# Dilated attention in a decoder layer: the segment scores as four wide products on TensorE in place of thirty-two 32x32 ones

## The reference

```python
x = layernorm(x + dilated_attention(x))          # 16 heads of 16, segments of 64, dilation 2
x = layernorm(x + cross_attention(x, ctx))       # 16 heads, causal, keys and values from ctx
x = layernorm(x + moe(x))                        # 32 experts, top 8, capacity, silu
```

```python
g = gather(x)                                    # [B, segment, head, 32, 16]
scores = einsum('bnhqd,bnhkd->bnhqk', g, g) * hd ** -0.5
out = einsum('bnhqk,bnhkd->bnhqd', softmax(scores), g)   # scattered back, 0 elsewhere
```

## Time and profile before

| what | value |
|---|---|
| median of 3 runs | 625.38 us (624.9 to 626.18) |
| span of the profiled execution | 719.4 us |
| PE busy, share of the span | 563.9 us, 78% |
| POOL busy | 390.5 us, 54% |
| DVE busy | 368.4 us, 51% |
| ACT busy | 330.1 us, 46% |

### The profile page before, as it was taken

The page is one execution under the profiler, slowest core; times in us unless marked ns, Lnnn a source line. Parts: engine busy times, 40 slices in busy tenths (PEclk is TensorE's granted clock), DMA queues, the critical chain, the costliest instruction groups (busy, mean ns, idle before and its releaser), DMA issues.

```text
span 719.4 us, 17476 instructions
## 1 busy us (share of the span) xinstructions
PE 563.9 (78%) x5097; PEld 414.4 (58%) x5098; DVE 368.4 (51%) x1527; ACT 330.1 (46%) x1204; POOL 390.5 (54%) x599
## 2 busy tenths in 40 slices
PE   3768787888878888888306889988998888985995
PEld 2445454544555554444105777777777776774884
DVE  1537566666677566666402444444444444443453
ACT  2445555455455455456003555555555554553012
POOL 5443445545544455545551666766666666665432
PEclk9789999999999899999556999999999999998899
DMA  9999996111111111112285554555555454554994
GB/s 206 277 275 365 342 339 231 69 59 73 68 50 64 55 73 73 65 66 74 99 308 182 155 165 150 160 156 167 152 164 159 143 157 142 164 160 148 425 418 145
DMA packets 83069, 121.31 MB, mean 169 GB/s; under 512 B 13779, under 2 KB 72669, under 8 KB 80992
## 3 DMA queue, kind: packets, MB, share of 16 engines
q1 hardware_dynamic: 64128, 78.46, 36.3%
q0 software_dynamic: 14016, 38.44, 14.7%
q10 hardware_dynamic: 4896, 4.03, 1.7%
HBM read 56.07 MB, written 69.01 MB: 174 GB/s over the span
## 4 chain that ended last, share of the span: by engine, by line
PE 54%; issue 12%; ACT 12%; DVE 9%; DMA 6%; ACTq 3%; POOL 2%; SPq 1%; another core or an unknown queue 0%; DVEq 0%; POOLq 0%
PE bank L793 14%; PE bank L809 9%; ACT pr L870 7%; PE bank L611 5%; PE bank L785 5%; PE bank L601 4%; PE bank L803 3%; PE bank L661 3%; DMA out<-fin 3%; PE bank L744 2%; DMA wall<-results 2%; DVE nmax L1024 2%; PE bank L619 2%; ACTq L296 1%; DVE tg L1218 1%
## 5 line engine op out<-in xcount | busy, mean ns | idle before, releaser
L556 POOL DMA_INDIRECT results<-ys,wcol x152 | 150.1, 988 | 25.8 <-POOL pscrap L545 22.0
L530 POOL DMA_INDIRECT queues<-x,xidx x128 | 129.1, 1009 | 36.9 <-issue 36.5
L793 PE MATMUL bank<-wall,xtT 128*128 x616 | 127.1, 330 | 0.7 <-issue 0.7
L870 ACT ACTIVATE pr<-bank,nmax 128x128 f32<-128x128 f32 x256 | 90.9, 370 | 29.1 <-DVE nmax L1024 29.1
L1218 DVE SCALAR_TENSOR_TENSOR tg<-th,bank 128x96 f32<-128x96 f32 x154 | 39.1, 254 | 125.3 <-ACT th L957 96.9
L793 PEld LDWEIGHTS bank<-wall,xtT 128*128 128x128 f32 x616 | 98.4, 194 | 1.4 <-issue 1.3
L963 ACT ACTIVATE ys<-bank,wcol 128x256 f32<-128x256 f32 x152 | 71.9, 473 | 54.6 <-PE bank L809 36.6
L809 PE MATMUL bank<-wall,hT 96*128 x304 | 94.5, 392 | 0.0
L785 PE MATMUL bank<-ident,xt 128*128 128x128 f32 x310 | 63.3, 286 | 35.4 <-DMA xt<-queues 24.1
L785 PEld LDWEIGHTS bank<-ident,xt 128*128 128x128 f32 x310 | 59.0, 197 | 49.9 <-DMA xt<-queues 25.1
L876 ACT COPY prT<-bank 128x512 f32<-128x512 f32 x64 | 38.5, 601 | 88.9 <-PE bank L611 86.2
(11 more groups left out here) (178 smaller groups left out, 947.2 us busy)
## 6 DMA issues: line engine op xcount, KB each, us to landing
xt<-queues SPq DMA_DIRECT2D x162, 160.0 KB
results<-zeros SPq DMA_DIRECT2D x16, 1024.0 KB
wall<-results SPq DMA_DIRECT2D x16, 1024.0 KB, 12.7
queues<-zeros SPq DMA_DIRECT2D x32, 160.0 KB, 4.9
wall<-in_L_ffn_w_gate SPq DMA_DIRECT2D x4, 768.0 KB
wall<-in_L_ffn_w_up SPq DMA_DIRECT2D x4, 768.0 KB
wall<-in_L_ffn_w_down SPq DMA_DIRECT2D x4, 768.0 KB
results<-ys,wcol POOLq DMA_INDIRECT x152
```

The source lines that it names most:

```text
L530: pool.indirect_dma_start(xg, bass.IndirectOffsetOnAxis(ap=xidx[:, par, k:k + 1], axis=0), x2[:, par, :], None, bounds_check=last_row, oob ...
L556: pool.indirect_dma_start(yr, bass.IndirectOffsetOnAxis(ap=wcol[:, u, 1:2], axis=0), ys[:, u, :], None, bounds_check=last_y, oob_is_err=Fa ...
L793: ins = pe.matmul(bank[2 + u % 2][:, 0:2 * INTER].rearrange("p (g i) -> p g i", g=2), xtT[:, u % 2, kk, :], wall[:, bass.ds(e, GU)].rearrange(
L870: ins = act.activation(pr[:, g % 2, q, :], pS[g % 2][:, q * P:(q + 1) * P], ACT.Exp, bias=nmax[:, 4 * g + q:4 * g + q + 1], accum_out=den[ ...
```

## The change

The scores of A are built from a folded and transposed `gm`. For each half `h` of the features (128 columns), PE multiplies `gm[:, half]` as weights with `fold`, a constant of 128x64 that adds the even and the odd token rows of a segment. Because each column of `gm` is zero in one of the two, the result `[128 features, 64]` holds every feature with its own tokens. ACT copies it from PSUM to `gF`. DVE then writes `gK` in one product: the same rows spread over four blocks, each feature only in the block of its own pair (`quarter` is that 0/1 mask). ACT writes the query rows `gQ` with two scaled copies, one for even and one for odd heads (`qmask` also carries the factor of 1/4, which leaves the exponentials' `scale`). The scores are then 4 products: weights of 128 rows and 64 columns, 128 moving columns. PE folds for tile `a+1` after the logits and before keys and values of tile `a`, and waits for the copy `gF` (`fold_out`, which ACT makes between the copies of T2 and of `x1`) before the transposes of `x1`. ACT makes the query rows (`query_rows`) after `vX` and before the copy of T3. DVE's product (`spread_x`) stands in the place of `turn_x`, which goes. The constants that this needs come before the first tile; their order on POOL changes, and the four pairs of masks of `qmask` move ahead of the first `mask_x`. The products of the probabilities with `gm` (L661) stay as they are.

```diff
-FIRST_CONST = 4
-B_CONST = FIRST_CONST + 23
-N_CONST = 49
+FIRST_CONST = 4 + 15
+B_CONST = FIRST_CONST + 14
+N_CONST = 55
...
+            put(pool.tensor_tensor, fold[:, :].rearrange("p (s i) -> p s i", s=2),
+                halves[:, :, 0, :], halves[:, :, 1, :], ALU.add)
+            put(pool.memset, qmask[:, :], float(HD) ** -0.5)
+            put(pool.memset, quarter[:, :], 0.0)
+            for g in range(NG):
+                rows = slice(GR * g, GR * (g + 1))
...
+                put(pool.memset, quarter[rows, g:g + 1], 1.0)
...
+            def folded(a, par):
+                pe.wait_ge(poolA.sem, poolA.at(a, "gm"))
+                for h in range(2):
+                    ins = pe.matmul(pX[:, D + SEG * h:D + SEG * (h + 1)], gm[:, par, h * P:(h + 1) * P], fold[:, :],
+                                    start=True, stop=True)
+                ins.then_inc(peG, 1)
...
-                for j in range(PAIRS):
-                    for g in range(NG):
-                        blk32 = gT[GR * g:GR * (g + 1), j * 32:(j + 1) * 32]
-                        ins = pe.matmul(pA[GR * g:GR * (g + 1), D + j * 32:D + (j + 1) * 32], blk32, blk32,
-                                        start=True, stop=True, tile_position=(GR * g, GR * g))
+                pe.wait_ge(actG.sem, actG.at(a, "query"))
+                for h in range(2):
+                    for k in range(2):
+                        ins = pe.matmul(pA[SEG * k:SEG * (k + 1), D + h * P:D + (h + 1) * P],
+                                        gQ[:, h, k, :, :].rearrange("p k i -> p (k i)"),
+                                        gK[:, 2 * h + k, :, :].rearrange("p j i -> p (j i)"),
+                                        start=True, stop=True, tile_position=(0, SEG * k))
...
+                if a is not None and not (isinstance(a, int) and a == NB - 1):
+                    folded(a + 1, 1 - par)
...
+                        pe.wait_ge(actG.sem, actG.at(a + 1, "fold"))
...
+            def fold_out(a):
+                act.wait_ge(peG, a + 1)
+                act.copy(gF[:, :, :].rearrange("p w i -> p (w i)"), pX[:, D:D + 2 * SEG]).then_inc(actG.sem, 1)
+            def query_rows(a):
+                act.wait_ge(actG.sem, actG.at(a, "fold"))
+                for k in range(DIL):
+                    ins = act.activation(gQ[:, :, :, k, :].rearrange("p h s i -> p (h s) i"), gF[:, :, :], ACT.Copy,
+                                         scale=qmask[:, k:k + 1])
...
-            def turn_x(a, par):
-                dve.wait_ge(poolA.sem, poolA.at(a, "gm"))
-                dve.transpose(gT[:, :], gm[:, par, :]).then_inc(dveA.sem, 1)
+            def spread_x(a):
+                dve.wait_ge(actG.sem, actG.at(a, "fold"))
+                dve.tensor_tensor(gK[:, :, :, :],
+                                  gF[:, :, :].unsqueeze(2)
+                                  .to_broadcast([P, 4, 4, GR]),
+                                  quarter[:, :].unsqueeze(1).unsqueeze(3).to_broadcast([P, 4, 4, GR]),
+                                  ALU.mult).then_inc(dveA.sem, 1)
```

More of the change, by code:

```diff
@@ L218, in build @@
         actX = Steps(sem("actX"), "r a")
-        dveA = Steps(sem("dveA"), "gT max sub sum inv turn scale add stats aggr")
+        dveA = Steps(sem("dveA"), "gK max sub sum inv turn scale add stats aggr")
+        peG = sem("peG")
+        actG = Steps(sem("actG"), "fold query")
         poolA = Steps(sem("poolA"), "gm ct")
@@ L424, in _ @@
             put(pool.memset, power[:, :], -0.5)
-            assert n == FIRST_CONST
+            halves = ident[:, :].rearrange("p (s k i) -> p s k i", s=2, k=DIL)
+            put(pool.tensor_tensor, fold[:, :].rearrange("p (s i) -> p s i", s=2),
[4 more added lines that the diff above has]
+                rows = slice(GR * g, GR * (g + 1))
+                for k, most in ((0, HD - 1), (1, -HD)):
+                    put(pool.affine_select, out=qmask[rows, k:k + 1], in_=qmask[rows, k:k + 1],
+                        compare_op=ALU.is_ge, fill=0.0, base=most, pattern=[[0, 1]],
+                        channel_multiplier=-1 if k == 0 else 1)
+                put(pool.memset, quarter[rows, g:g + 1], 1.0)
+            assert n == FIRST_CONST, n
             put(pool.memset, own[:, :], 0.0)
@@ L437, in _ @@
             put(pool.memset, causal[:, :], 0.0)
-            put(pool.memset, qmask[:, :], float(HD) ** -0.5)
             put(pool.tensor_copy, identb[:, :], ident[:, :])
@@ L441, in _ @@
                 rows = slice(GR * g, GR * (g + 1))
-                for k, most in ((0, HD - 1), (1, -HD)):
-                    put(pool.affine_select, out=qmask[rows, k:k + 1], in_=qmask[rows, k:k + 1],
-                        compare_op=ALU.is_ge, fill=0.0, base=most, pattern=[[0, 1]],
-                        channel_multiplier=-1 if k == 0 else 1)
                 put(pool.affine_select, out=causal[rows, :], in_=causal[rows, :], compare_op=ALU.is_ge,
@@ L695, in step @@
                 if a is not None:
+                    if not (isinstance(a, int) and a == NB - 1):
+                        pe.wait_ge(actG.sem, actG.at(a + 1, "fold"))
                     pe.wait_ge(dveN.sem, dveN.at(a, "x1"))
@@ L882, in exps_A @@
                 act.wait_ge(dveA.sem, dveA.at(a, "sub"))
-                act.activation(flat2(eA[:, :, :]), flat2(sA[:, :, :]), ACT.Exp, scale=float(HD) ** -0.5
-                               ).then_inc(actA.sem, 1)
+                act.activation(flat2(eA[:, :, :]), flat2(sA[:, :, :]), ACT.Exp).then_inc(actA.sem, 1)
+            def fold_out(a):
[6 more added lines that the diff above has]
+                                         scale=qmask[:, k:k + 1])
+                ins.then_inc(actG.sem, 1)
             def turned_context(a):
@@ L903, in step @@
                     probs_T(b, 2)
+                if a is not None and not (isinstance(a, int) and a == NB - 1):
+                    fold_out(a + 1)
                 if a is not None:
@@ L921, in step @@
                              pC[:, D:2 * D].rearrange("p (j s c) -> p j s c", s=2, c=HD)).then_inc(actA.sem, 1)
+                if a is not None and not (isinstance(a, int) and a == NB - 1):
+                    query_rows(a + 1)
                 if b is not None:
```

16 lines of the change are left out of this document (12 added, 4 removed).

## The result

The changed kernel takes 635.8 us (median of 4 runs, 635.29 to 638.52) against 625.78 us of the kernel before beside it (4 runs, 624.9 to 626.59): ratio 1.0175, 95% interval 1.0150 to 1.0199. It is slower, and the time is inside the stated range, 4.8 us above the 631.0 forecast. The profiled execution took 635.4 us with a span of 633.7.

What follows compares the result with a forecast made beforehand. The prediction took a ring through several engines to bound part one's step, with PE's profiled stall absent from timed runs. 625.4 + 6.0 (15 steps of 0.4) - 0.4 (start) = 631.0 us, range 605 to 638.

Steps and rivals of the forecast that it cites:

- the ring of a step: Part one: a dependency loop through PE, DVE, POOL and ACT, claimed to bound each step in timed runs.
- the likeliest case: Timed runs have no stall at L661 and the additions make steps slower: 631.0 us, own range 627 to 637, chance 0.55.
- Sum for a step: 0.4 us, between 0 and 0.65: Part one: net added time per step from all parts of the change; +6.0 us for 15 steps, between 0 and +9.8.
- the spread +0.25: DVE's 512-element product replacing L1040's 256: 0.69 us against 0.44, so +0.25 us a step, low end 0.
- The start: Before and in the first tile: constants about even, longer first tile, masks out of the way; -0.4 us, between -1 and +1.
- If DVE is what is late, the +0.25, if PE is, the +0.4; both in a row 0.65: Part one's step: spread on DVE or folding on PE reaches the ring; in a row 0.65 us less the slack left.
- DVE becomes the bound: Rival: folding, wait and spread in a row cost 0.65 to 1 us a step, 635 to 640 us; chance 0.1.
- The 94 us: Gap between profiled span 719.4 and median 625.4 us, taken to show that timed runs don't pay PE's stall at L661.
- The recording of them holds PE back: PE's bursts of small products at L661 and L640: profiling causes the 38.7 us stall, so timed runs don't pay it.
- the span would come down to about 675 us: Profiled execution after the change: span 30 to 50 us shorter than 719.4, as the stall at L661 shrinks.
- The slack of DVE before `ew`: DVE's wait for ACT before the router's weights, 0.64 us a step in the profile, counted as nearly none without the stall.
- The additions are hidden: Rival: POOL's `root_a` clocks the step, covering PE's 0.4 us while DVE fills a gap; 625 us, chance 0.1.

Runs made afterwards that it cites:

- b_fold: Kernel before plus the two folding products on PE alone, written to columns nobody reads; 632.21 us, ratio 1.0112.
- a_mask: Changed kernel with one more wait, so POOL's `gm` product starts only after DVE's `pickb`; 633.01 us, ratio 1.0118.
- b_wide_mask: Kernel before plus an unused 512-element DVE product in front of `gT`, with POOL's mask product waiting for `pickb`; 632.44 us, ratio 1.0123.
- a_idx: Changed kernel with the index of the scatters written before maxima 0 instead of behind them; 636.2 us, ratio 1.0166.
- a_idle_mask: Changed kernel with folding, copy, spread and query rows moved a tile ahead into idle time, plus POOL's wait for `pickb`; 640.54 us, ratio 1.0247.

## Why the prediction was right or wrong

**The direction and the place were right; the branch that pays, and the size, were not.** The kernel is slower because what the change adds lies on the ring of a step, as the likeliest case said. The forecast had 5.6 us, and the timed ratio makes 10.9 (0.0175 x 625.4). The step that failed is "Sum for a step: 0.4 us, between 0 and 0.65", which is 0.80 measured: twice the value, and above its upper end. Its 0.4 was the folding on PE. The runs show 0.6 of DVE's branch (the wait for `gF` and the longer spread) and 0.2 of `pickb` meeting `gm`; the folding alone would cost 0.41 (b_fold), but it lies beside DVE's longer branch and is covered by it. That a slower kernel was forecast from the shorter branch is in part luck.

What stood wrong in that sum:

1. *The wait for `gF` was named and not priced.* The prediction says of the spread that it "also waits for `gF`, while L1040 waited for nothing", but gives the copy 0 and the spread +0.25. The folding ends 0.5 us behind `x1`'s start, and the copy comes behind that, so DVE waits 0.35 us. DVE's branch grows by 0.43 (wait and start) + 0.24 (length) = 0.67 us, not by 0.25, and is the longer one. a_mask, with nothing else added, has +0.60 a step; b_wide_mask, with 0.69 us of other work in the same place, +0.55.
2. *`pickb` against `gm` was not foreseen.* It is 0.2 us a step on average (a_mask, 17.29 to 17.08). In the steps where they meet, `pickb` lasts until `gm` is done (158.79 and 158.74). The Trainium skill (SBUF — State Buffer, Who interferes with whom) says that VectorE and GpSimd share a pair of ports under an exclusive lock, and that a `tensor_scalar` can need it. The trace agrees: 0.81 us beside `gm`'s 0.74 where it is 0.18 alone, and 0.18 again in a_idx with the same starts, where by that rule `pickb` had the pair first.
3. *The start* was costed at -0.4 us and is +0.4 (the first `oT` at 44.47 against 44.11).

What offset a part: of the 15 tiles taken at 0.4, 13 pay and two don't (9.6 + 0.6 - 0.35 = 9.9 us in all). With the start's 0.4 that is 10.2 us (the last `oT` at 297.00 against 286.78), inside the 9.4 to 12.4 of the timed ratio.

**"If DVE is what is late, the +0.25, if PE is, the +0.4; both in a row 0.65"** had the right alternatives. b_fold gives PE's alone +0.41 us. But both are full at once in the kernel before, so neither has slack to speak of (`er` ends 0.07 us before `ew` starts), and they don't add up: both together are +0.55, as DVE's alone. The rival "DVE becomes the bound", 635 to 640 us at 0.65 to 1 us a step with a chance of 0.1, is the one that came true, in its engine and in size. Its "in a row" holds for the wait and the spread; the folding stands in that row only through the wait for `gF`, and 0.2 of the 0.80 us are the meeting, which it did not have.

**The 94 us.** "The recording of them holds PE back" was wrong. Recorded once more, the same kernel shows no stall, and bursts of 64 in 1.00 us (L661) and 0.75 us (L640). That the timed runs don't stall was right, but in part by luck, since the reason was wrong: it was one odd execution, whose expert loop was 39 us longer too, where the program is the same. What disturbed it, no run here tells. With it goes the claim that the span would come down to about 675 us: it is 633.7, above the 623.3 of the kernel before. The slack of DVE before `ew`, 9.0 us in 14 steps, was also the odd execution's: the second profile has 0.6 us in 13 steps.

**Single terms.** Four score products take 0.59 us from their start to the next one (161.83 to 162.42), where 0.45 was taken and the old ones had 0.68: PE then waits for `oT` all the same, 15.3 us in 13 steps against 14.0 for the 32. Folding is 0.47 us from its start to the next product (155.37 to 155.84), where 0.4 was taken and 0.45 was the upper bound. `gF` has 0.27 us, the spread 0.69, both as taken. The query rows are 0.69 to 0.75 us, above the 0.55 given as their most, and cost nothing where they stand; a_idle_mask shows them cost 0.57 us where ACT is awaited. "No idle PE before L698" is right. The folding is not covered by a late `root_a`: `x1` waits 0.8 us for it before and after, and PE's 0.47 us still come through (+0.41 in b_fold), which the rival "The additions are hidden" had needed.

**Open** stay the odd execution's cause, why a few hundredths of a microsecond decide between `pickb` and `gm`, and what the ring would give back if both branches were shorter.

## What to carry to other kernels

When a stage is a ring through several engines, list each way from the last common instruction to the next one (here `x1` and `ew`) with its length, before and after: what is added to parallel ways costs what it adds to the longest of them, and a wait of a moved consumer for its new producer is a term of that sum like any instruction. A product that replaces 32 others is worth what the ring waits for it at that place, here nothing. And a profile whose span lies far from the timed median is no basis for a price or a slack: profile the same kernel again first, and read untouched stages of both.

## What the runs showed of the hardware

- The same program was profiled once with a span of 719.4 us, its 32x32 products stalled in every step, and once with 623.3, without the stall; the spans of its timed runs beside the experiments lie between 621.4 and 626.6. A single profile can be such an execution.
- 64 records of 32x32 products take 0.68 us, and 8 of the wide form (128 rows, 64 weight columns, 128 moving) 0.59 us: less than a tenth of a microsecond between them.
- A DVE instruction of 32 elements takes 0.18 us. With POOL's product of 256 elements (0.74 us) starting 0.02 us behind it, it takes 0.81 us in some steps and 0.18 in others of the same profile (a_idx). It is held by a scatter of POOL's too: starting 0.54 us into its 0.97 us, it ended with it after 0.45 us, while in the kernel before it starts 0.27 us into it (152.77 and 152.50) and takes 0.18.
- DVE's float32 product of two SBUF operands to 512 elements takes 0.69 us whether it reads a folded tile by broadcasting or another (0.68).
